# Graph message passing on one core: one gathered unit fewer in each round, two rounds more, and 5 of 21 key one-hots made by ScalarE

## The chip, the cores and the metric

The kernel runs on one core of a Trainium2 chip. The metric is the device time of one execution in microseconds (us); lower is better. The engines are named as the profile names them: PE is TensorE (PEld its weight loads), DVE is VectorE, ACT is ScalarE, POOL is GpSimd, SP is SyncE.

## The reference

```
x: [12500, 64]   src, dst: [400000], dst sorted ascending   edge_attr: [400000, 64]   edge_weight: [400000, 1]
h   = x @ node_w.T
rf  = edge_attr @ review_w.T
m   = (h[src] + rf) * edge_weight
agg = segment_sum(m, dst, 12500)
out = layernorm(x + agg)          # over the 64 features
```

Since both products are linear, the kernel first sums `weight * x[src]` and `weight * edge_attr` per destination node into `sums` (128 partitions: 64 features of x, 64 of edge_attr; one column per node), and multiplies by the two weight matrices once at the end.

## The kernel before

**Two ways to sum x[src].** Edges are sorted by destination. For the first 90 units of 2048 edges (`ROUNDS * GATHERED` = 18 x 5) the rows `x[src]` are gathered from memory by indirect DMA, 16 DMAs of 128 rows to a unit, issued by POOL (`gather_tiles`, L534). PE then sums the gathered rows and the unit's edge_attr rows with a weighted one-hot (`sum_g`), and DVE adds the result to `sums` (`add_g`). For the nodes of all later edges nothing of x is gathered. Those nodes are taken three at a time, as a *span*: one run of 128 edges per span. DVE makes two one-hots of the run (`make_hot`): `hot_key`, 128 edges x 294 keys (L854), where the key is `(src >> 7) * 3 + (dst - first node)`, and `hot_lo`, the low 7 bits of src times the weight, in two parts (L855). PE multiplies them (`count_window`, L1425) into a table of weights per source and node, ACT copies two spans' tables from PSUM to `counts` (`read_counts`, L1240), and PE multiplies `counts` with the resident table of x (`sum_x`, L1438). DVE adds that into `sums` (`add_x`, L772). The edge_attr rows of these later edges come by plain DMAs in 106 units, six to a round (`SUMMED`), summed by `sum_a`, `multiply_a`, `add_a`.

**Rounds and steps.** A round is 6 steps (`RG`), a step is a group of 21 spans (`GW`). 18 rounds of 126 spans cover the last 6804 nodes, and 8 spare spans (`SPILLS`) take runs longer than 128 edges. Rounds run in a hardware loop of two rounds to an iteration, and the last two rounds stand outside it. Step g of a round multiplies counts of group g while the spans of group g+1 are made and counted; in steps 0 to 4 it also has one gathered unit, in every step one edge_attr unit.

**The order on each engine is written out by hand**, in `step_of` of each engine:

- PE: spans 0 to 20 of the next group, with `sum_g` ahead of span 4, `multiply_g` ahead of 8, `sum_a` ahead of 12, `multiply_a` ahead of 16, and a fifth of `sum_x` ahead of each of 4, 8, 12, 16 and 20. The small transposes (`turn_g`, `turn_a`, `turn_cols`) stand ahead of 8 in steps 1, 2 and 4.
- DVE: six spans ahead of PE, since each one-hot has six buffers (`HOT_BUFS`) and waits `counted` for the span six before; the step's other work (`make_g_hot`, `make_a_hot`, `make_..._slot_hot`, `add_g`, `add_a`) lies between the spans, and `add_x` ends the step.
- ACT: the 11 copies of a step (`read_counts`), with `copy_g` after the second, `copy_a` after the sixth, and once a round `compare` (step 0, L1215), `read_g`, `read_a` and `read_cols`. PE may not start a pair of spans before the copy of the pair two before is done.
- POOL: for the round after, `gather_row`, `gather_unit` 0, `gather_runs`, `gather_unit` 1 to 4, all in one queue. `gather_row` (L552) fetches the 128 edges that hold the begin of each run; it follows `find_rows` on DVE (L793, step 0) and `find_runs` on DVE (L802, step 1, ahead of the loop's k = 22) waits for it. `gather_unit` 0 also waits for `take_src` on DVE (L706, step 1, k = 14), and each unit waits until PE has summed the unit that held its buffer in the round before.

## Time and profile before

| what | value |
|---|---|
| time, median of 3 runs | 2291.5 us (2286.46 to 2296.65) |
| the profiled execution: its time | 2279.48 us |
| the profiled execution: its span | 2277.7 us |
| mean granted TensorE clock | 0.915 of full |
| busy DVE | 1986.1 us, 87% |
| busy PE | 1891.5 us, 83% |
| busy POOL | 1674.5 us, 74% |
| busy ACT | 962.4 us, 42% |
| instructions | 93210 |

The span is the time from the first to the last instruction. A busy share counts only the time within instructions: POOL, in a row of indirect DMAs, is not busy in the pause between two of them, and matmuls overlap, so a busy PE is not one at its peak. "Issue" is time in which an engine waited for nothing that the profile shows. Rows of a timeline give start, duration, engine, line, instruction, and in brackets the idle time before and what ended it.

### The profile page before, as it was taken

What the parts mean: (1) busy time and instruction counts of PE and PEld (TensorE: products, weight loads), DVE (VectorE), ACT (ScalarE), POOL (GpSimd) and SP (SyncE); (2) the same over time, 40 slices, a digit from 0 to 9 for tenths busy, and PEclk for the clock granted to TensorE, in tenths of its full rate; (3) what the DMA queues carried; (4) which work ended last, traced back from release to release, by engine and by line L of the source; (5) the groups of instructions that cost most, each with busy time, mean ns of one, the idle gap of its engine ahead of it and who ended that gap; (6) DMA issues with size and microseconds to landing.
All of it is one profiled execution on the core that took longest, in us unless ns stands there. A gap on an engine that the chain in (4) does not pass through costs nothing.

```text
span 2277.7 us, 93210 instructions
## 1 busy us (share of the span) xinstructions
PE 1891.5 (83%) x35999; PEld 1641.8 (72%) x36000; DVE 1986.1 (87%) x6206; ACT 962.4 (42%) x1602; POOL 1674.5 (74%) x1539
## 2 busy tenths in 40 slices
PE   1659788979897989898998899789988998989974
PEld 1557677767776777777777778677777877877864
DVE  3969898989898989898998899889988998989974
ACT  0324344444344444444443445344434443444434
POOL 3777777777777777777777777777777777777700
PEclk8679998999898999999998999899988998989997
DMA  6224333433333333333333333333433333433302
GB/s 139 55 59 86 72 79 79 83 72 83 78 74 76 84 77 84 76 84 77 84 76 76 76 85 80 75 72 84 84 75 69 82 79 71 84 73 72 66 3 57
DMA packets 480104, 173.08 MB, mean 76 GB/s; under 512 B 443549, under 2 KB 455397, under 8 KB 479445
## 3 DMA queue, kind: packets, MB, share of 16 engines
q1 hardware_dynamic: 426791, 111.57, 22.8%
q0 software_dynamic: 49632, 51.95, 11.4%
q8 instruction: 314, 5.14, 1.0%
q10 hardware_dynamic: 3218, 3.20, 0.7%
q14 instruction: 149, 1.22, 0.2%
HBM read 163.39 MB, written 3.20 MB: 73 GB/s over the span
## 4 chain that ended last, share of the span: by engine, by line
POOL 67%; issue 20%; DVE 7%; PE 2%; DMA 1%; ACT 1%; DVEq 0%; POOLq 0%; ACTq 0%; SPq 0%
POOL rows L534 64%; DVE hot_lo L855 3%; DVE hot_key L854 2%; DMA counts<-dst 1%; POOL run_src L560 1%; POOL run_dst L560 1%; POOL run_w L560 1%; POOL dst_row L552 1%; PE x_ps L1438 1%; ACT x_tab L1308 1%; DMA dst_row<-dst,row_i 0%; PE count_ps L1425 0%; DVE packed L990 0%; PE count_ps L1451 0%; DVE x_tab L1010 0%
## 5 line engine op out<-in xcount | busy, mean ns | idle before, releaser
L534 POOL DMA_INDIRECT rows<-x,g_src_cols x1440 | 1584.3, 1100 | 443.6 <-issue 438.7
L1240 ACT ACTIVATE counts<-count_ps 128x588 f32<-128x588 f32 (+1 forms) x1192 | 851.9, 750 | 1138.3 <-PE count_ps L1425 1127.5
L1425 PE MATMUL count_ps<-hot_key,hot_lo 128*128 128x294 f32 x4552 | 897.9, 330 | 257.2 <-DVE hot_lo L855 213.0
L855 DVE SCALAR_TENSOR_TENSOR hot_lo<-count,cols 128x256 fp32r<-128x256 f16 x2276 | 1078.6, 474 | 0.0
L1425 PEld LDWEIGHTS count_ps<-hot_key,hot_lo 128*128 128x128 f32 x4552 | 673.6, 196 | 386.7 <-DVE hot_lo L855 247.5
L854 DVE TENSOR_SCALAR hot_key<-count,cols 128x294 fp32r<-128x294 f16 x2276 | 864.5, 380 | 47.8 <-PE count_ps L1425 27.7
L1438 PE MATMUL x_ps<-counts,x_tab 128*64 128x63 f32 x21364 | 800.2, 229 | 41.3 <-DVE sums L772 41.2
L1438 PEld LDWEIGHTS x_ps<-counts,x_tab 128*64 128x64 f32 x21364 | 725.6, 142 | 102.5 <-DVE sums L772 48.0
L1352 PE MATMUL unit_ps<-rows,g_hot 128*32 128x64 f32 x5760 | 120.8, 246 | 0.0
L1352 PEld LDWEIGHTS unit_ps<-rows,g_hot 128*32 128x32 f32 x5760 | 104.4, 127 | 18.2 <-issue 18.2
L802 DVE TENSOR_SCALAR off<-dst_row,b_all 126x128 f32<-126x128 int32 x18 | 5.2, 290 | 116.4 <-DMA dst_row<-dst,row_i 116.4
L662 POOL TENSOR_TENSOR x_tab<-x_tab,counts 128x512 f32<-128x512 f32 (+1 forms) x6 | 5.5, 937 | 91.7 <-DVE counts L1021 91.7
L1352 PE MATMUL unit_ps<-rows,a_hot 128*32 128x64 f32 x3392 | 69.3, 222 | 0.0
L1352 PEld LDWEIGHTS unit_ps<-rows,a_hot 128*32 128x32 f32 x3392 | 52.2, 109 | 17.7 <-issue 17.7
L772 DVE TENSOR_TENSOR sums<-sums,x_ps 64x63 f32 (+1 forms) x216 | 47.0, 218 | 13.2 <-PE x_ps L1438 6.3
L1223 ACT ACTIVATE g_slots<-unit_ps 128x128 f32<-128x128 f32 x90 | 25.0, 278 | 58.9 <-PE unit_ps L1352 58.9
L1389 PE MATMUL window_bank<-a_slot_hot,a_slots 128*64 128x128 f32 x212 | 45.8, 298 | 0.0
L744 DVE TENSOR_SCALAR a_slot_hot<-column,a_slot_dst 128x128 f32<-128x128 f32 x106 | 40.6, 383 | 3.3
L1381 PE MATMUL window_bank<-g_slot_hot,g_slots 128*128 128x128 f32 x180 | 36.3, 283 | 0.0
L552 POOL DMA_INDIRECT dst_row<-dst,row_i x18 | 18.3, 1017 | 24.3 <-DVE row_i L796 19.1
L1451 PE MATMUL count_ps<-w_t,sums 128*128 128x128 f32 x196 | 24.9, 296 | 12.8 <-DVEq L1187 12.8
L1451 PEld LDWEIGHTS count_ps<-w_t,sums 128*128 128x128 f32 x196 | 24.8, 212 | 12.9 <-DVEq L1187 12.9
(196 smaller groups left out, 728.3 us busy)
## 6 DMA issues: line engine op xcount, KB each, us to landing
rows<-edge_attr SPq DMA_DIRECT2D x196, 512.0 KB
rows<-x,g_src_cols POOLq DMA_INDIRECT x1440
out<-x_tab SPq DMA_DIRECT2D x12, 256.0 KB
counts<-dst SPq DMA_DIRECT2D x1, 848.0 KB
a_stage<-dst SPq DMA_DIRECT2D x17, 48.0 KB
a_stage_w<-edge_weight SPq DMA_DIRECT2D x17, 48.0 KB
g_stage<-src SPq DMA_DIRECT2D x18, 40.0 KB
g_stage<-dst SPq DMA_DIRECT2D x18, 40.0 KB
```

What stands on the lines that cost most here:

```text
L534: pool.indirect_dma_start(out=g_x[:, i, t, :], out_offset=None, in_=x, in_offset=bass.IndirectOffsetOnAxis(ap=g_src_cols[at.p][:, k:k + 1] ...
L552: pool.indirect_dma_start(out=dst_row[:, :], out_offset=None, in_=dst.rearrange("(a b) -> a b", b=P), in_offset=bass.IndirectOffsetOnAxis( ...
L560: pool.indirect_dma_start(out=tile, out_offset=None, in_=dram.rearrange("(a b) -> a b", b=1), in_offset=bass.IndirectOffsetOnAxis(ap=index ...
L772: made = dve.tensor_tensor(to, to, x_ps[half * F:(half + 1) * F, 0:NS], ALU.add)
L854: dve.tensor_scalar(hot_key[h][:, :], count16[:, :], cols_[:, KEY, j:j + 1], None, ALU.is_equal)
L855: dve.scalar_tensor_tensor(hot_lo[h][:, :, :], count16[:, 0:P].unsqueeze(1).to_broadcast([P, 2, P]), cols_[:, LO, j:j + 1], cols_[:, W_LOW ...
L1240: act.activation(to, count_ps[(g + e) % 2][:, 0:n, 0:KEYS].rearrange("p a (h d) -> p a h d", d=D), ACT.Copy).then_inc(counts_read, 1)
L1352: done = pe.matmul(to[j * PAD:(j + 1) * PAD, :], hot[:, at:at + PAD], tiles[:, q * QUADS + j, :], start=(q == 0), stop=(q == STACK - 1))
L1389: pe.matmul(a_window_ps, a_slots[:, :], a_slot_hot[:, :], start=True, stop=True).then_inc(a_multiplied, 1)
L1425: done = pe.matmul(count_ps[(g + e) % 2][:, k % 2, 0:KEYS], hot_lo[h][:, i, :], hot_key[h][:, :], start=(i == 0), stop=(i == 1))
L1438: done = pe.matmul(x_ps[half * F:(half + 1) * F, 0:n], x_tab[:, hi, :], counts[:, g % 2, hi, 0:n], start=(hi < 2), stop=(hi >= HI - 2))
L1451: last = pe.matmul(out_ps[n % 2][:, i, :], sums[:, (h0 + i) * P:(h0 + i + 1) * P], w_t[:, :], start=True, stop=True)
```

## The change

`ROUNDS` goes from 18 to 20 and `GATHERED` from 5 to 4. So 80 units of edges are gathered instead of 90, the edge_attr units that are not gathered go from 106 to 116 (two of them in the last round, where there were four), and 2528 spans are counted instead of 2276. In each step, five of the 21 spans (1, 5, 9, 13 and 17) get their `hot_key` from ACT: `far_key = |count - key|` in one activation (Abs, with the negated key as bias), then `hot_key = relu(1 - far_key)` in a second (Relu, with a column of ones as bias), which waits for the first. DVE leaves out L854 for these spans and still makes their `hot_lo`. `read_cols` writes the negated keys once a round, and PE waits for `act_key_ready` besides `hot_ready` ahead of these spans. ACT makes the key of span 2e+6 or 2e+7 behind the copy of pair e.

```diff
--- before.py
+++ after.py
@@ -34,11 +34,12 @@
 D = 3
 GW = 21
 RG = 6
-ROUNDS = 18
-GATHERED = 5
+ROUNDS = 20
+GATHERED = 4
 SUMMED = 6
 SPILLS = 8
 HOT_BUFS = 6
+ACT_KEYS = (1, 5, 9, 13, 17)
 ATTR_BUFS = 2
 NOWHERE = 1000.0
 
@@ -156,6 +157,8 @@
         KEY, LO, W_LOW, W_TOP = range(CELLS)
         packed = sb("packed", [P, CELLS, P])
         cols = [sb(f"cols{b}", [P, CELLS, RW]) for b in range(2)]
+        neg_key = [sb(f"neg_key{b}", [P, RW]) for b in range(2)]
+        far_key = sb("far_key", [P, KEYS], F16)
         hot_key = [sb(f"hot_key{b}", [P, KEYS], F32R) for b in range(HOT_BUFS)]
         hot_lo = [sb(f"hot_lo{b}", [P, 2, P], F32R) for b in range(HOT_BUFS)]
 
@@ -303,6 +306,8 @@
         added = sem("added")
 
         hot_ready = sem("hot_ready")
+        far_made = sem("far_made")
+        act_key_ready = sem("act_key_ready")
         counted = sem("counted")
         counts_read = sem("counts_read")
         x_summed = sem("x_summed")
@@ -851,7 +856,8 @@
                     dve.wait_ge(cols_ready, at.r + g // RG + 1)
                 if not isinstance(n, int) or n >= HOT_BUFS:
                     dve.wait_ge(counted, n - HOT_BUFS + 1)
-                dve.tensor_scalar(hot_key[h][:, :], count16[:, :], cols_[:, KEY, j:j + 1], None, ALU.is_equal)
+                if k not in ACT_KEYS:
+                    dve.tensor_scalar(hot_key[h][:, :], count16[:, :], cols_[:, KEY, j:j + 1], None, ALU.is_equal)
                 dve.scalar_tensor_tensor(
                     hot_lo[h][:, :, :], count16[:, 0:P].unsqueeze(1).to_broadcast([P, 2, P]), cols_[:, LO, j:j + 1],
                     cols_[:, W_LOW:W_TOP + 1, j].unsqueeze(2).to_broadcast([P, 2, P]), ALU.is_equal, ALU.mult
@@ -1205,8 +1211,41 @@
             def read_cols(q, p, n=RW):
 
                 act.wait_ge(turned, q + 1)
+                act.activation(neg_key[p][:, 0:n], turn_ps[:, KEY * n:(KEY + 1) * n], ACT.Copy, scale=-1.0)
                 act.activation(cols[p][:, :, 0:n], turn_ps[:, 0:CELLS * n].rearrange("p (q t) -> p q t", q=CELLS), ACT.Copy
                                ).then_inc(cols_ready, 1)
+
+            def keys_before(at, g, k):
+
+                return (at.r * RG + g) * len(ACT_KEYS) + sum(i < k for i in ACT_KEYS)
+
+            def make_key(at, g, k):
+
+
+                h, j = (g * GW + k) % HOT_BUFS, (g % RG) * GW + k
+                n, made = first(at, g) + k, keys_before(at, g, k)
+                neg = neg_key[at.p if g < RG else 1 - at.p]
+                if g % RG == 0 and k == ACT_KEYS[0]:
+                    act.wait_ge(cols_ready, at.r + g // RG + 1)
+                if not isinstance(n, int) or n >= HOT_BUFS:
+                    act.wait_ge(counted, n - HOT_BUFS + 1)
+                if not isinstance(made, int) or made >= 1:
+                    act.wait_ge(act_key_ready, made)
+                act.activation(far_key[:, :], count16[:, :], ACT.Abs, bias=neg[:, j:j + 1]).then_inc(far_made, 1)
+                act.wait_ge(far_made, made + 1)
+                act.activation(hot_key[h][:, :], far_key[:, :], ACT.Relu, bias=all_ones[:, 0:1], scale=-1.0
+                               ).then_inc(act_key_ready, 1)
+
+            def keys_after(at, g, e):
+
+
+                for ahead in (2 * e + HOT_BUFS, 2 * e + HOT_BUFS + 1):
+                    at_g, at_k = g + ahead // GW, ahead % GW
+                    over = isinstance(at.r, int) and at.r * RG + at_g > ROUNDS * RG
+                    if e == EVACS - 1 and ahead > 2 * e + HOT_BUFS:
+                        continue
+                    if at_k in ACT_KEYS and not over and at_k < windows_of(at, at_g):
+                        make_key(at, at_g, at_k)
 
             def compare(q):
 
@@ -1259,8 +1298,12 @@
             act.wait_ge(tables_ready, 1)
             with act.If(is_narrow(act) == 1):
                 read_cols(0, 0)
+                for w in ACT_KEYS:
+                    if w < HOT_BUFS:
+                        make_key(Round(0, 0), 0, w)
                 for e in range(EVACS):
                     read_counts(Round(0, 0), 0, e)
+                    keys_after(Round(0, 0), 0, e)
 
                 def step_of(at, g):
 
@@ -1270,6 +1313,12 @@
                     for e in range(EVACS):
                         if e < evacs:
                             read_counts(at, c, e)
+                            if not (last and c == RG):
+                                keys_after(at, c, e)
+                            else:
+                                for ahead in (2 * e + HOT_BUFS, 2 * e + HOT_BUFS + 1):
+                                    if ahead in ACT_KEYS and ahead < SPILLS:
+                                        make_key(at, c, ahead)
                         if e == 1 and g < GATHERED:
                             copy_g(at, g)
                         if e == 2 and g == 0 and not last:
@@ -1417,6 +1466,8 @@
                 n, h = first(at, g) + k, (g * GW + k) % HOT_BUFS
                 e = k // 2
                 pe.wait_ge(hot_ready, n + 1)
+                if k in ACT_KEYS:
+                    pe.wait_ge(act_key_ready, (at.r * RG + g) * len(ACT_KEYS) + ACT_KEYS.index(k) + 1)
                 if k % 2 == 0:
                     before = evacs_before(at, g) + e
                     if not isinstance(before, int) or before >= 2:
```

## Rows read from the trace of the kernel before

**Rows 1.** The page: busy time of each engine, and the chain by engine.

```profile
PE 1891.5 (83%) x35999; PEld 1641.8 (72%) x36000; DVE 1986.1 (87%) x6206; ACT 962.4 (42%) x1602; POOL 1674.5 (74%) x1539
...
POOL 67%; issue 20%; DVE 7%; PE 2%; DMA 1%; ACT 1%; DVEq 0%; POOLq 0%; ACTq 0%; SPq 0%
```

**Rows 2.** Waits, all engines: total us, times, longest.

```profile
POOL rows L534 <- issue: 438.7, 1439, 0.3
...
DVE off L802 <- DMA dst_row<-dst,row_i: 116.4, 18, 21.3
```

**Rows 3.** Groups by line: count, busy us, mean ns, idle before.

```profile
L534 POOL DMA_INDIRECT rows<-x,g_src_cols x1440 | 1584.3, 1100 | 443.6 <-issue 438.7 <-DVE g_src_cols L706 4.9
...
L855 DVE SCALAR_TENSOR_TENSOR hot_lo<-count,cols 128x256 fp32r<-128x256 f16 x2276 | 1078.6, 474 | 0.0
...
L1240 ACT ACTIVATE counts<-count_ps 128x588 f32<-128x588 f32 (+1 forms) x1192 | 851.9, 750 | 1138.3 <-PE count_ps L1425 1127.5
...
L854 DVE TENSOR_SCALAR hot_key<-count,cols 128x294 fp32r<-128x294 f16 x2276 | 864.5, 380 | 47.8 <-PE count_ps L1425 27.7 <-issue 18.7 <-ACT cols L1208 0.7
...
L1215 ACT ACTIVATE compared<-sample_tab,bias_all 126x1696 bf16<-126x1696 int16 x18 | 30.4, 1691 | 0.0
...
L1308 ACT ACTIVATE x_tab<-x_tab,counts 128x64 f32<-128x64 f32 x56 | 13.4, 333 | 0.0
...
L1195 ACT ACT_TABLE_LOAD x1 | 1.3, 1283 | 6.3 <-PE turn_ps L1322 6.3
```

**Rows 4.** VectorE timeline, markers of a round (start us, us, engine line).

```profile
45.97 0.29 DVE L802 TENSOR_SCALAR off<-dst_row,b_all 126x128 f32<-126x128 int32 x1 [5.97 <-DMA dst_row<-dst,row_i]
...
98.33 0.15 DVE L793 TENSOR_SCALAR less<-less 126x1 f32<-126x1 f32 x1 [1.13 <-ACT compared L1215]
...
145.76 0.29 DVE L802 TENSOR_SCALAR off<-dst_row,b_all 126x128 f32<-126x128 int32 x1 [21.27 <-DMA dst_row<-dst,row_i]
...
1994.25 0.14 DVE L793 TENSOR_SCALAR less<-less 126x1 f32<-126x1 f32 x1
...
2028.99 0.29 DVE L802 TENSOR_SCALAR off<-dst_row,b_all 126x128 f32<-126x128 int32 x1 [8.66 <-DMA dst_row<-dst,row_i]
```

**Rows 5.** VectorE timeline, the adds that end a step.

```profile
1045.45 0.21 DVE L772 TENSOR_TENSOR sums<-sums,x_ps 64x63 f32 x1
...
1069.34 0.47 DVE L772 TENSOR_TENSOR sums<-sums,x_ps 64x63 f32 x2
...
1108.36 0.21 DVE L772 TENSOR_TENSOR sums<-sums,x_ps 64x63 f32 x1
...
1125.80 0.21 DVE L772 TENSOR_TENSOR sums<-sums,x_ps 64x63 f32 x1
...
1145.39 0.21 DVE L772 TENSOR_TENSOR sums<-sums,x_ps 64x63 f32 x1
...
1161.58 0.47 DVE L772 TENSOR_TENSOR sums<-sums,x_ps 64x63 f32 x2
```

**Rows 6.** VectorE timeline, consecutive instructions.

```profile
1071.78 0.36 DVE L854 TENSOR_SCALAR hot_key<-count,cols 128x294 fp32r<-128x294 f16 x1
1072.07 0.47 DVE L855 SCALAR_TENSOR_TENSOR hot_lo<-count,cols 128x256 fp32r<-128x256 f16 x1
1072.46 0.26 DVE L715 TENSOR_TENSOR g_hot<-column,g_cols 128x112 f32<-128x112 f32 x1
```

**Rows 7.** Windows, one step: length, then busy of PE, PEld, DVE, ACT, POOL.

```profile
874.25:891.71 17.46, 16.37 (x352) 14.08 (x343) 17.23 (x53) 8.23 (x14) 13.50 (x14) 1.00 0.43 89
```

**Rows 8.** TensorE timeline, start of a step.

```profile
873.36 1.11 PE L1352 MATMUL unit_ps<-rows,g_hot 128*32 128x64 f32 x64
874.78 1.38 PE L1438 MATMUL x_ps<-counts,x_tab 128*64 128x63 f32 x38 [0.30 <-DVE sums L772]
876.08 1.35 PE L1425 MATMUL count_ps<-hot_key,hot_lo 128*128 128x294 f32 x8
877.27 0.39 PE L1381 MATMUL window_bank<-g_slot_hot,g_slots 128*128 128x128 f32 x2
```

## The prediction

> **What bounds the kernel now.** I read the page first. VectorE (DVE) has the highest busy share, 87%, TensorE (PE) has 83%, GpSimd (POOL) 74% [rows 1]. But the chain that ended last runs through POOL for 67% of the span and through "issue" for another 20% [rows 1]. The list of waits explains the second part: POOL's gathers were preceded 1439 times by some 0.3 us of issue, 438.7 us in all [rows 2]. Busy and idle of L534 together are 1584.3 + 443.6 = 2027.9 us over 1440 gathers, 1.408 us each [rows 3]. So POOL has no free time, although its busy share says a quarter. A round of POOL is 80 gathers and 4 small ones, which I price alike: 84 x 1.408 = 118.3 us. The markers of a round on DVE give the same: from the first L793 of the loop to the last there are 16 rounds in 1994.25 - 98.33 = 1895.9 us, 118.5 us each [rows 4].
>
> Who pays is seen in DVE's wait at L802 for the row gather, which stands behind all gathers of the round before in POOL's queue: 116.4 us in 18 waits [rows 2]. Of these 5.97 us lie before and 8.66 us behind the 16 rounds, so 101.8 us lie within them [rows 4]. Without these waits the round would have been (1895.9 - 101.8) / 16 = 112.1 us. This is the pace of DVE with PE close behind it, and POOL hides it. So the kernel has two bounds, 118.3 us (POOL) and 112.1 us (DVE), and both must fall for the time to fall per round. The change adds two rounds: it has to win more than a tenth of each round to win at all.
>
> In the 112.1 us there is one more thing. The step at the seam of the hardware loop, from 1045.45 to 1069.34, takes 23.9 us [rows 5], against some 17.5 us for its kind; a plain step with a gathered unit takes 17.44 us (1108.36 to 1125.80) and the last step of a round, which has no gathered unit, 16.19 us (1145.39 to 1161.58) [rows 5]. So a seam costs 6.4 us in every second round, or 3.2 us a round. I leave it as it is: nothing in the change touches it, and the number of seams rises with the rounds.
>
> **The change part by part.**
>
> *Gathers.* A round has 64 instead of 80: (64 + 4) x 1.408 = 95.7 us on POOL. The first gathered unit of the next round also waits for the source columns (L706, step 1, k = 14); from there POOL needs 95.7 us up to and with the next row gather, and L802 of the next round stands 8 spans behind that round's L706. So POOL stalls nobody so long as a round is longer than about 96 us. It will then wait for DVE, not DVE for it. The wait of 5 to 6 us a round at L802 goes away; what is late next is DVE's own sequence. The start fits too: the first big wait, 21.27 us at 145.76 [rows 4], was for 80 gathers behind each other; 16 fewer end 22.5 us earlier.
>
> *Keys on DVE.* In a row of spans, L855 starts 0.29 us after L854, and the next instruction 0.39 us after L855 [rows 6]; the means of 380 and 474 ns [rows 3] hold overlap at their ends. A removed key is worth the spacing, 0.29 us. 30 keys a round: 8.7 us. Bounds: 0.38 us, its whole duration, if nothing overlapped (11.4 us a round), and 0.21 us, if two L855 in a row can't overlap (0.29 less 0.474 - 0.39), 6.3 us.
>
> *One gathered unit less on DVE.* The steps with and without it differ by 17.44 - 16.19 = 1.25 us [rows 5].
>
> So DVE's pace is 112.1 - 8.7 - 1.25 = 102.2 us a round.
>
> *PE.* Its work in a span, a portion of `sum_x` and so on is unchanged in a round, and it loses the sums of one gathered unit. In the step from 874.25 to 891.71 it is busy for 16.37 of 17.46 us at a granted clock of 1.00 [rows 7], but that contains stretches in which it waited for DVE within a group. From the starts: a portion of `sum_x` takes 1.30 us (874.78 to 876.08), four spans 1.2 us (876.08 to 877.27), a gathered unit 1.1 us (873.36, then 0.30 us idle before 874.78) [rows 8]. Five portions, 21 spans at 0.30 to 0.32 us, 1.1, and about 1.1 us of smaller products and switches give 15.1 to 15.5 us, an estimate of the floor of a step; 16.37 is the ceiling. DVE's plain step becomes 17.44 - 5 x 0.29 = 16.0 us. So the two engines, a tenth apart before, are nearly level afterwards, and each will sometimes wait for the other across the six buffers.
>
> *Keys on ACT.* The trace has no Abs or Relu. Its two rows with a per-partition operand are 64 columns in 333 ns and 1696 columns in 1691 ns [rows 3]; between them 0.832 ns a column, so 294 columns take 524 ns. The second activation waits for the first, so a key takes 1.05 us; the bounds are 0.9 us, if the activations overlap at their ends by 0.08 us as DVE's instructions do [rows 6], and 1.3 us, if each hand-over costs another 0.1 us. A step has 5 keys, 5.3 us. ACT was busy for 8.23 us in a step [rows 7], so 13.5 us of 16.0 us, and 15.4 us in step 0 with `compare` (1.69 us and its read-out). It holds, but it is no longer free at once when PE has counted a pair. The place that I expect to matter: the key behind the copy of pair 8 puts 1.05 us between the copies of pairs 8 and 9, and PE needs the copy of pair 9 for the first pair of the next step, after one portion of `sum_x` and one span (1.6 us). ACT needs 0.2 + 0.7 + 1.05 + 0.7 us from the count of pair 8, PE arrives 0.65 + 1.6 us after it: 0.4 us short. In DVE's pace this lies in time that PE has left (16.0 less 15.5 us). The negated keys, one activation of some 0.3 us a round, are on no path.
>
> The rule of the Trainium skill, "ScalarE: Activation LUTs", section "Rules for kernel authors", speaks against such a move: relu and the like belong on VectorE, not on ScalarE. The rows bear out its premise, 0.29 us on DVE against about 1.05 us on ACT for a key; by it alone the change would cost 0.76 us for each of 600 keys, 456 us of engine time, but on an engine with more than half of its time free [rows 1]. The sum goes by which engine sets the step.
>
> *Coupling.* For DVE and PE being level, for ACT's copies coming later, for `compare` coming later to L793 (DVE waited 1.13 us there already [rows 4]) I put 1.5 us a round on top. Bounds: 0, as everything now goes by DVE, and 6 us, 1 us a step, if PE stands at its ceiling of 16.37 us and ACT's 0.4 to 0.6 us come on top. I take the low part, since a step of PE at its ceiling contains waits that go with DVE's pace. The round is then 103.7 us.
>
> **The sum.** Before: 98.3 us to the first L793, 16 x 118.5 = 1895.9, and 283.5 us from the last L793 to the end (2277.7 - 1994.25); together 2277.7. After: the start falls by 1.3 us (five keys of the first group go to ACT), 97.0. Then 18 rounds of 103.7 us, 1866.6. The last part loses the wait of 8.66 us at 2028.99 [rows 4], some 60 keys (17.4 us) and two edge_attr units of the last round (4 x 0.6 us and their tail, 2 us net), and gains the coupling of nearly two rounds: 283.5 - 8.7 - 17.4 - 2.0 - 2.5 for the two gathered units + 2.5 = 255.4 us. Span: 2219 us. About 2 us lie around the span (2279.48 against 2277.7), and the median of the runs is 13.8 us above the span before; at the same ratio, 1.0061, the median after is 2232 us. In short form the span is 145 + 20 x round, and it equals that of before at a round of 106.6 us.
>
> **The rivals.**
>
> *TensorE becomes the bound.* Against it: DVE's list of waits holds little for PE in plain steps, and its step of 17.44 us is far above PE's floor. For it: 16.37 us busy at full clock [rows 7] is above the new 16.0 us. Six steps at 16.4 to 16.5 us, with DVE's long steps (1 and 4) unchanged, add about 2 us: a round of 105.5 us, 2269 us. If it is a little more, 106.6 us, nothing is gained.
>
> *ScalarE's keys hold up TensorE's copies: slower.* One mechanism: PE must wait for the copy of pair 9 (and in step 0 for that of pair 3 behind `compare`), falls behind DVE, and DVE waits for `counted`. The price is what exceeds PE's reserve. From 0.8 us a step on (106.6 less 102.2 over six steps, rounded up) the change is lost; at 1.15 us a step the round is 109 us and the time 2339 us. For it: ACT's share in step 0 is 15.4 of 16 us. Against: ACT falls behind by 0.4 to 0.6 us in my sum, once a step, and catches up.
>
> *Table loads.* If Abs or Relu were not in the loaded set, two loads of 1.283 us [rows 3] would come with every key: 77 us a round, ACT would then set a round of some 160 us, and the time would be over 3300 us. The trace shows one load for Identity, Copy and Sign together, at L1195, and says nothing of the other two. The Trainium skill, "ScalarE: Activation LUTs", section "Table sets: the hidden batching unit", says that relu and abs are in every set; by that this rival is out.
>
> *The relief is larger.* The removed key is worth 0.38 us, or DVE never waits for PE, because with the row waits gone PE keeps the granted clock of 1.00 that it has in the plain step [rows 7], where its mean is 0.915. The round is 100 to 101 us and the time 2160 to 2180 us.
>
> *No relief.* POOL stays the bound: only if a gather became slower than 1.408 us by a tenth or more, which nothing here suggests, since it waits for neither DVE nor data.
>
> **How the numbers follow.** DVE sets the pace with some coupling (2202 to 2268 us, round 102.2 to 105.5): 0.60, likeliest 2232. TensorE sets it, still faster (about 2269): 0.14. Between (round 106.0 to 107.2): 0.05. ScalarE holds up TensorE (about 2339): 0.09. Larger relief (about 2180): 0.10. Table loads or POOL: 0.02. A difference of under 0.5%, 11 us, is about what a measurement of this kernel can't tell from no change; that is 2280 to 2303 us. Faster: 0.60 + 0.14 + 0.10 = 0.84; same 0.05; slower 0.11. The range is 2185 to 2295 us: it leaves out the larger half of the larger relief and the slower cases, less than 0.2 together.
>
> **What the profile would show.** Right: DVE's wait at L802 near zero; POOL idle some 5 us or more in each round, waiting for L706; L854 1926 times, L855 2528 times, 0.39 us apart where they follow each other; a round of 102 to 105 us from L793 to L793; the activations at 0.52 us each; no further table load; ACT busy near 75%; a plain step near 16 us; PE's granted clock above 0.915, as the long waits are gone. Wrong: a plain step above 17 us with DVE waiting for `count_ps` in every step, and PE waiting for ACT's `counts` or keys: then the coupling was the term that failed. If L855 behind L855 takes 0.47 us, it was the key's price. If the seam's cost grows, because ACT now restarts late as well, it was the term that I left unchanged.

## The result, and the profile after

The changed kernel takes 2263.84 us (median of 4 runs, 2262.61 to 2268.77), the kernel before 2289.68 us (median of 4). The ratio on record is 0.9895, 95% interval 0.9865 to 0.9925; the two medians alone give 0.9887. It is faster, and the time lies in the range, but the gain is 1.05% where 2.6% was forecast. The profiled execution has a span of 2266.8 us; the sum had said 2219.

The page after, busy shares and the chain by engine, against [rows 1]:

```profile
PE 1983.5 (88%) x38569; PEld 1752.4 (77%) x38570; DVE 1987.5 (88%) x6186; ACT 1578.5 (70%) x2973; POOL 1703.4 (75%) x1387
...
DVE 39%; PE 29%; issue 16%; POOL 5%; DVEq 4%; ACT 4%; DMA 2%; ACTq 0%; SPq 0%; POOLq 0%
```

The chain moved from POOL (67%) to DVE and PE (39% and 29%). From this alone one would say that POOL is out of it. The groups by line say otherwise, against [rows 3]:

```profile
L539 POOL DMA_INDIRECT rows<-x,g_src_cols x1280 | 1605.7, 1254 | 406.5 <-issue 383.1 <-DVE g_src_cols L711 22.2 <-DVE row_i L801 1.2
...
L861 DVE SCALAR_TENSOR_TENSOR hot_lo<-count,cols 128x256 fp32r<-128x256 f16 x2528 | 1165.8, 476 | 0.1
...
L860 DVE TENSOR_SCALAR hot_key<-count,cols 128x294 fp32r<-128x294 f16 x1926 | 722.6, 375 | 73.5 <-PE count_ps L1476 72.1 <-ACT cols L1215 0.9
...
L1236 ACT ACTIVATE hot_key<-far_key,all_ones 128x294 fp32r<-128x294 f16 x602 | 326.1, 542 | 19.6
...
L1234 ACT ACTIVATE far_key<-count,neg_key 128x294 f16<-128x294 f16 x602 | 316.2, 525 | 0.1
```

Each gather of x rows became longer: 1254 ns in the mean instead of 1100. Busy and idle are now 1605.7 + 406.5 us; without the 23.4 us in which POOL waited for L711 and L801 that is 1.55 us a gather instead of 1.41, 10% more. 64 gathers and 4 small ones are then 105.6 us, where 95.7 us was forecast. The waits, against [rows 2]:

```profile
DVE hot_key L860 <- PE count_ps L1476: 72.1, 40, 6.3
...
DVE off L807 <- DMA dst_row<-dst,row_i: 67.5, 12, 15.0
...
DVE less L798 <- ACT compared L1254: 30.5, 20, 6.1
...
POOL rows L539 <- DVE g_src_cols L711: 22.2, 19, 5.2
```

The wait for the row gather, now L807, is 67.5 us instead of 116.4; it was to vanish. POOL itself waited only 22.2 us in all for DVE (L711), about 1 us a round: it has almost no slack. The markers of a round (L798, L793 before), against [rows 4]:

```profile
92.42 0.15 DVE L798 TENSOR_SCALAR less<-less 126x1 f32<-126x1 f32 x1 [0.95 <-ACT compared L1254]
...
960.48 0.15 DVE L798 TENSOR_SCALAR less<-less 126x1 f32<-126x1 f32 x1 [1.42 <-ACT compared L1254]
...
1171.83 0.15 DVE L798 TENSOR_SCALAR less<-less 126x1 f32<-126x1 f32 x1 [1.42 <-ACT compared L1254]
...
2009.77 0.15 DVE L798 TENSOR_SCALAR less<-less 126x1 f32<-126x1 f32 x1 [1.21 <-ACT compared L1254]
```

From the first to the last there are 18 rounds in 1917.35 us, 106.5 us each; the forecast was 103.7. The two rounds in the middle, 960.48 to 1171.83, take 105.7 us each; over most of the kernel the rounds take 98.4 and some 113.4 us in turn, and the mean also holds two early ones of 115.2 and 117.3 us. Within the 18 rounds DVE waits 55.3 us for the row gather (67.48 less the first wait of 5.94 and the last of 6.20), 3.1 us a round. The adds that end a step, against [rows 5]:

```profile
946.26 0.47 DVE L777 TENSOR_TENSOR sums<-sums,x_ps 64x63 f32 x2
...
971.74 0.47 DVE L777 TENSOR_TENSOR sums<-sums,x_ps 64x63 f32 x2
...
1005.42 0.47 DVE L777 TENSOR_TENSOR sums<-sums,x_ps 64x63 f32 x2
...
1021.17 0.47 DVE L777 TENSOR_TENSOR sums<-sums,x_ps 64x63 f32 x2
...
1052.60 0.21 DVE L777 TENSOR_TENSOR sums<-sums,x_ps 64x63 f32 x1
...
1070.08 0.21 DVE L777 TENSOR_TENSOR sums<-sums,x_ps 64x63 f32 x1
```

A plain step takes 15.75 us (1005.42 to 1021.17), even less than the 16.0 us of the forecast. The step at the seam of the loop takes 25.48 us (946.26 to 971.74), against 17.48 us for the same step without a seam (1052.60 to 1070.08). This seam is the shortest of the eight within the loop; their mean is 26.0 us.

### The profile page after: what moved, and what is told of

Its sections match the earlier page's. It is cut to its first block, busy times and chain, and to the rows that moved or that the text cites. A ratio compares the mean times of both kernels' runs of the same rounds, so it can differ in the third digit from the quotient of the medians.

```text
span 2266.8 us, 102339 instructions
## 1 busy us (share of the span) xinstructions
PE 1983.5 (88%) x38569; PEld 1752.4 (77%) x38570; DVE 1987.5 (88%) x6186; ACT 1578.5 (70%) x2973; POOL 1703.4 (75%) x1387
## 4 chain that ended last, share of the span: by engine, by line
DVE 39%; PE 29%; issue 16%; POOL 5%; DVEq 4%; ACT 4%; DMA 2%; ACTq 0%; SPq 0%; POOLq 0%
DVE hot_lo L861 19%; PE count_ps L1476 12%; PE x_ps L1489 12%; DVE hot_key L860 11%; POOL rows L539 5%; PE unit_ps L1401 4%; DMA dst_row<-dst,row_i 2%; ACT compared L1254 1%; DVEq L764 1%; DVE sums L777 1%; ACT counts L1279 1%; DMA counts<-dst 1%; DVEq L858 1%; DVE sums L767 1%; DVEq L755 1%
## 5 line engine op out<-in xcount | busy, mean ns | idle before, releaser
L539 POOL DMA_INDIRECT rows<-x,g_src_cols x1280 | 1605.7, 1254 | 406.5 <-issue 383.1
L1279 ACT ACTIVATE counts<-count_ps 128x588 f32<-128x588 f32 (+1 forms) x1324 | 922.4, 744 | 550.6 <-PE count_ps L1476 547.0
L861 DVE SCALAR_TENSOR_TENSOR hot_lo<-count,cols 128x256 fp32r<-128x256 f16 x2528 | 1165.8, 476 | 0.1
L1476 PEld LDWEIGHTS count_ps<-hot_key,hot_lo 128*128 128x128 f32 x5056 | 727.5, 193 | 280.9 <-issue 110.1
L1489 PE MATMUL x_ps<-counts,x_tab 128*64 128x63 f32 x23716 | 871.2, 226 | 20.1 <-DVE sums L777 20.0
L1489 PEld LDWEIGHTS x_ps<-counts,x_tab 128*64 128x64 f32 x23716 | 788.8, 139 | 87.4 <-issue 33.0
L860 DVE TENSOR_SCALAR hot_key<-count,cols 128x294 fp32r<-128x294 f16 x1926 | 722.6, 375 | 73.5 <-PE count_ps L1476 72.1
L1236 ACT ACTIVATE hot_key<-far_key,all_ones 128x294 fp32r<-128x294 f16 x602 | 326.1, 542 | 19.6
L1234 ACT ACTIVATE far_key<-count,neg_key 128x294 f16<-128x294 f16 x602 | 316.2, 525 | 0.1
L1401 PE MATMUL unit_ps<-rows,g_hot 128*32 128x64 f32 x5120 | 105.6, 243 | 0.0
L807 DVE TENSOR_SCALAR off<-dst_row,b_all 126x128 f32<-126x128 int32 x20 | 5.6, 281 | 67.5 <-DMA dst_row<-dst,row_i 67.5
L767 DVE TENSOR_TENSOR sums<-sums,window_bank 64x128 f32 x116 | 33.9, 293 | 4.1
L1438 PEld LDWEIGHTS window_bank<-a_slot_hot,a_slots 128*64 128x64 f32 x232 | 22.2, 134 | 19.7 <-issue 19.7
L1254 ACT ACTIVATE compared<-sample_tab,bias_all 126x1856 bf16<-126x1856 int16 x20 | 36.5, 1825 | 0.0
```

The lines of the kernel that those rows point to most:

```text
L539: pool.indirect_dma_start(out=g_x[:, i, t, :], out_offset=None, in_=x, in_offset=bass.IndirectOffsetOnAxis(ap=g_src_cols[at.p][:, k:k + 1] ...
L860: dve.tensor_scalar(hot_key[h][:, :], count16[:, :], cols_[:, KEY, j:j + 1], None, ALU.is_equal)
L861: dve.scalar_tensor_tensor(hot_lo[h][:, :, :], count16[:, 0:P].unsqueeze(1).to_broadcast([P, 2, P]), cols_[:, LO, j:j + 1], cols_[:, W_LOW ...
L1234: act.activation(far_key[:, :], count16[:, :], ACT.Abs, bias=neg[:, j:j + 1]).then_inc(far_made, 1)
L1236: act.activation(hot_key[h][:, :], far_key[:, :], ACT.Relu, bias=all_ones[:, 0:1], scale=-1.0).then_inc(act_key_ready, 1)
L1254: act.activation(compared[:, :], sample_tab[0:RW, :], ACT.Sign, bias=bias_all[:, bass.ds(q, 1)], accum_out=less[:, 0:1]).then_inc(compared ...
```

## Where the gathers lose their time

The lengths of single gathers in the trace after fall into groups: most of 0.94 to 1.1 us, then 78 between 1.7 and 2.9 us, and 39 of more than 5 us, 19 of them in step 4, 19 in step 5 (one each in 19 of the 20 rounds) and one near the start. One of them, from step 5, on POOL, and the two instructions on DVE near its end (start us, us, engine, line):

```profile
933.97 6.22 POOL L539 DMA_INDIRECT rows<-x,g_src_cols  x1 [0.30 <-issue]
...
939.11 0.27 DVE L720 TENSOR_TENSOR a_hot<-column,a_cols 128x112 f32<-128x112 f32 x1
...
939.41 0.28 DVE L722 TENSOR_TENSOR a_hot<-a_hot,a_cols 128x112 f32<-128x112 f32 x1
```

L722 waits for L720, so DVE is idle for 0.03 us ahead of it (instructions that follow each other without a wait overlap by some 0.1 us instead). The gather ends at 940.19 us, 0.78 us after L722 starts. The same is found in the kernel before:

```profile
1180.18 3.11 POOL L534 DMA_INDIRECT rows<-x,g_src_cols  x1 [0.30 <-issue]
...
1182.21 0.26 DVE L715 TENSOR_TENSOR g_hot<-column,g_cols 128x112 f32<-128x112 f32 x1
...
1182.50 0.28 DVE L717 TENSOR_TENSOR g_hot<-g_hot,g_cols 128x112 f32<-128x112 f32 x1
```

It ends at 1183.29 us, 0.79 us after the start of L717. Of the 117 long gathers after and the 78 before (over 1.7 us), 116 and 77 end 0.7 to 0.8 us after the start of an instruction of DVE that follows an idle gap (L717, L706, L753 and L762 before; the last three read PSUM). For gathers below 1.3 us such an instruction lies 0.45 to 0.95 us ahead of the end in only 260 of 1358 cases before and 273 of 1120 after. So a long gather seemed to be waiting for DVE to pause. Step 4 has no gathered unit any more, so no `make_g_hot` and no `add_g` between its spans: from k = 6 to k = 18 twelve spans follow each other without a pause, where there were two pauses before. Step 5 never had a gathered unit, and its stream was as unbroken in the kernel before; what changed there is that keys left it.

## The experiments

Theory A: the gather is held up by DVE until DVE pauses. Theory B: the lengths come from POOL's own queue or place in the round. Theory C: the seams are on the path. Rival D to C: POOL takes it back. The ratios are those on record, to the kernel before as it ran beside each (medians of 2285.4 to 2289.7 us), with 95% intervals.

| run | what | time us | ratio | mean gather ns |
|---|---|---|---|---|
| change | | 2263.84 | 0.9895 (0.9865 to 0.9925) | 1254 |
| e1_rounds_only | rounds part alone | 2339.73 | 1.0230 (1.0196 to 1.0263) | 1148 |
| e2_keys_only | keys part alone | 2374.86 | 1.0389 (1.0345 to 1.0433) | 1173 |
| e3_pauses | change, 5 pauses in steps 4, 5 | 2226.42 | 0.9736 (0.9708 to 0.9764) | 1105 |
| e8_one_pause | change, 1 pause in steps 4, 5 | 2216.02 | 0.9697 (0.9666 to 0.9728) | 1168 |
| e10_no_pause | change, 5 waits without pause | 2264.49 | 0.9898 (0.9879 to 0.9917) | 1257 |
| e6_before_pauses | before, 4 pauses a step | 2235.95 | 0.9789 (0.9756 to 0.9822) | 1037 |
| e4_long_loop | change, 6 rounds an iteration | 2262.89 | 0.9906 (0.9873 to 0.9939) | 1264 |
| e5_both | e3 and e4 together | 2177.01 | 0.9523 (0.9495 to 0.9550) | 1104 |
| e7_compare_early | e5, compare moved ahead | 2172.86 | 0.9505 (0.9473 to 0.9536) | 1125 |
| e9_before_both | before, e6 and 4 rounds an iteration | 2214.11 | 0.9675 (0.9656 to 0.9695) | 1042 |
| e11_one_pause_all | e7 with 1 pause | 2165.45 | 0.9464 (0.9446 to 0.9482) | 1171 |

### Pauses in the streams of steps 4 and 5

```diff
+PAUSES = (8, 10, 12, 14, 16)
 # VectorE, step_of
                     for k in range(HOT_BUFS, GW + HOT_BUFS):
+                        if g >= GATHERED and k in PAUSES and not last:
+                            dve.wait_ge(hot_ready, first(at, c) + k)
```

> The changed kernel, but VectorE waits for its own previous hot_lo ahead of five of the spans (k = 8, 10, 12, 14, 16) in steps 4 and 5, which makes a pause of about 0.1 us each. Theory A: a gather gets in at any pause, so the gathers of 5.5 and 6.2 us shrink to under 3 us, the mean falls from 1.25 to about 1.12 us, the waits for the row gather (67.5 us) fall to some 25 us, those of the first rounds, and the time to about 2235 us, 0.976 of before. Theory B: gathers and time as in the changed kernel (0.9895), plus 1 us a round for the pauses.

Measured: 2226.42 us. The group of POOL's gathers, and two of the waits:

```profile
L540 POOL DMA_INDIRECT rows<-x,g_src_cols x1280 | 1414.5, 1105 | 544.2 <-issue 384.3 <-DVE g_src_cols L712 159.9
```

```profile
POOL rows L540 <- DVE g_src_cols L712: 159.9, 19, 15.3
...
DVE off L808 <- DMA dst_row<-dst,row_i: 20.9, 2, 15.0
```

Ten waits more a round on DVE made the kernel 37 us faster. All but one of the gathers above 5 us are gone (one of 12 us at the start is left), POOL has 159.9 us to wait for DVE, and the row gather is waited for in two early rounds only. Without the time in which POOL waited for DVE a gather now costs (1414.5 + 544.2 - 159.9) / 1280 = 1.405 us, the 1.408 us of the prediction. The round is 104.1 us (99.6 and 108.6, from L799 to L799), next to the forecast 103.7. The pauses have their price on DVE: each is an idle gap of 0.13 us, and steps 4 and 5 take 18.0 and 15.75 us instead of 16.8 and 14.65 to 14.85 us, some 2.2 us a round and not the 1 us that was expected.

### The same waits without a pause

```diff
-                            dve.wait_ge(hot_ready, first(at, c) + k)
+                            dve.wait_ge(hot_ready, first(at, c) + k - 2)
```

> The same five waits in steps 4 and 5 as in the first test with pauses, but each for the hot_lo two spans earlier, which is long done: the instructions and their number are the same, VectorE does not pause. Theory A (the pause lets the gather in): gathers of 5.5 and 6.2 us as in the changed kernel, time 0.99. Rival (the wait instructions themselves, or the shift in code, helped): 0.974.

```profile
L540 POOL DMA_INDIRECT rows<-x,g_src_cols x1280 | 1609.4, 1257 | 404.6 <-issue 383.4 <-DVE g_src_cols L712 20.0 <-DVE row_i L802 0.9
```

```profile
DVE off L808 <- DMA dst_row<-dst,row_i: 67.3, 12, 16.2
```

Measured: 2264.49 us, 39 gathers above 5 us, the wait for the row gather as in the changed kernel. With the same instructions and no pause nothing is gained. It is the pause that ends a gather's wait.

### One pause instead of five

`PAUSES = (12,)`.

> The changed kernel with a single pause, at k = 12 of steps 4 and 5. Theory A: any pause that comes in the stream ends a gather's wait, so the longest waits are halved, below 3.5 us, and the time is near that with five pauses (0.974), at most 0.98. If what matters is the whole of the pauses, and not one in the middle, 0.985 or more.

```profile
L540 POOL DMA_INDIRECT rows<-x,g_src_cols x1280 | 1494.9, 1168 | 454.1 <-issue 382.8 <-DVE g_src_cols L712 69.7 <-DVE run_i L814 0.6
```

Measured: 2216.02 us, 10 us better than with five. The gathers of 5.5 and 6.2 us are cut to 1.8 and 2.5 us; the mean is longer than with five pauses, but DVE loses less in the two steps (17.0 and 14.8 or 15.2 us instead of 18.0 and 15.7), and POOL is still just fast enough: the row gather is waited for about 1 us in every second round. The two runs were made on different chips, and the intervals of their ratios overlap, so that one pause is better than five is likely and not shown.

### Pauses in the kernel before

The same two lines in the kernel before, in all six steps, with `PAUSES = (7, 12, 17, 21)`.

> The kernel before, with nothing of the change, but VectorE waits for its own previous hot_lo ahead of the spans at k = 7, 12, 17 and 21 of each step. Theory A (a gather gets in only at a pause of VectorE) says that waits on VectorE make this kernel faster: the gathers of 2.1 to 3.1 us shrink, the mean falls from 1.10 to about 1.05 us, a round from 117.1 to about 114 us, where VectorE's own 112.1 us and 2.4 us of pauses set it; ratio about 0.98. Rival (the gathers' length has nothing to do with VectorE, the pauses in the other test worked by moving something else): no change, or slower by what the pauses cost, 1.00 to 1.02.

```profile
L535 POOL DMA_INDIRECT rows<-x,g_src_cols x1440 | 1493.6, 1037 | 472.5 <-issue 434.9 <-DVE g_src_cols L707 36.4 <-DVE row_i L797 0.9
```

Measured: 2235.95 us, ratio 0.9789. Against [rows 3] the mean fell from 1100 to 1037 ns, and 3 gathers instead of 78 are above 1.7 us. The round is 116.0 us instead of 118.5 (about 114 was expected), and DVE waits for the row gather in two early rounds only. A gather now costs (1493.6 + 472.5 - 36.4 - 0.9) / 1440 = 1.339 us: of the 1.408 us that the prediction took for POOL's own price, a part was already time held up by DVE. In a kernel that POOL bounds, waits on an engine that is 87% busy are worth 2.1%, twice what the whole change is. Theory A stands for the kernel before as well.

### The rounds part alone

`ACT_KEYS = ()`: 20 rounds of 4 gathered units, all keys on DVE.

> 20 rounds with 4 gathered units, all keys on VectorE (the rounds part of the change alone). Theory of the sum: VectorE's work is about 106.5 us a round (107.8 before less 1.25), with seams and compare about 111 us, POOL free; time about 2385 us, 1.04 of before. Theory A (a gather is held up by VectorE's streams with lone L861 behind each other): no gather above 3.6 us here, mean back at 1.10 us. Theory B (the long gathers come from POOL's own queue with 64 gathers a round, or from steps 4 and 5 having no gathered unit): two gathers of 5 to 6 us a round here too, mean 1.25 us. The seam: if the keys on ScalarE made it dearer, TensorE's issue pause at it is back at some 4.6 us; if not, 6.8 us.

```profile
L539 POOL DMA_INDIRECT rows<-x,g_src_cols x1280 | 1470.1, 1148 | 613.0 <-issue 382.5 <-DVE g_src_cols L711 229.0 <-DVE row_i L801 0.9
```

Measured: 2339.73 us, ratio 1.023. POOL waits 229.0 us for L711: here DVE sets the pace, 110.5 us a round (106.7 and 114.2 in turn). The round is as expected, the time 45 us below the 2385 us that were made of it. Neither theory was right about the gathers. Theory A expected none above 3.6 us: there are 18 above 5 us (16 of them 6.4 us) with all keys on DVE. Theory B expected two in each round and a mean of 1.25 us: there is one, and the mean is 1148 ns. 16 of the 18 lie in step 4, the step that lost its pauses. Step 5, whose stream is without a pause for its first 8.4 us here and in the kernel before, has one above 5 us in 20 rounds here and none there. So a stream without a pause is not enough by itself. As to the seam: TensorE's pauses at it (`count_ps`, issue) come to 5.1 us in the mean, against 6.5 us in the changed kernel, and the step at it takes 7.1 us more than without a seam, against 8.6 us. The keys on ACT made the seam dearer.

### The keys part alone

18 rounds of 5 gathered units, keys of five spans on ACT; `compared` and `far_key` share memory, for space, with two more waits on ACT.

```diff
-ROUNDS = 20
-GATHERED = 4
+ROUNDS = 18
+GATHERED = 5
-        compared = sb("compared", [RW, SAMPLES], BF16)
+        scratch = sb("scratch", [P, SAMPLES + KEYS % 2], BF16)
+        compared = scratch[0:RW, 0:SAMPLES]
-        far_key = sb("far_key", [P, KEYS], F16)
+        far_key = scratch[:, 0:KEYS].bitcast(F16)
```

> 18 rounds with 5 gathered units, keys of 5 spans on ScalarE (the keys part alone; the scratch of compare and far_key share memory, for space, which adds a short wait on ScalarE). The kernel stays bound by POOL, so VectorE's 8.7 us a round give nothing: 1.00. By theory A the lone L861 make the streams harder to get into, the gathers longer and the kernel slower: mean above 1.15 us, 84 gathers a round, 4 us or more a round, 1.02 to 1.04.

```profile
L540 POOL DMA_INDIRECT rows<-x,g_src_cols x1440 | 1689.4, 1173 | 443.3 <-issue 438.6 <-DVE g_src_cols L712 4.7
```

```profile
DVE off L808 <- DMA dst_row<-dst,row_i: 343.4, 18, 33.7
```

Measured: 2374.86 us, ratio 1.0389, and the wait for the row gather is 343.4 us against 116.4 [rows 2]. DVE's work fell and the kernel became 3.9% slower: 80 gathers x 0.073 us are 5.8 us a round, times 18 some 105 us; the span grew by 96 us. The forecast of theory A, 1.02 to 1.04, held. Neither part is a gain by itself. Together they are, since the one takes gathers off POOL and the other work off DVE.

The two halves also tell where each long gather comes from. Mean gather in ns, and in brackets how many are above 5 us, sorted by the step in which the gather starts (from the timelines of POOL and DVE):

| run | step 4 | step 5 |
|---|---|---|
| before | 1118 (0) | 1042 (0) |
| rounds part alone | 1736 (16) | 1109 (1) |
| keys part alone | 1151 (0) | 1832 (17) |
| change | 1764 (19) | 1807 (19) |

The gather in step 5 of the keys part alone is that of the changed kernel, and it ends behind the same instruction of DVE (L723 here, L722 there):

```profile
1200.05 6.21 POOL L540 DMA_INDIRECT rows<-x,g_src_cols  x1 [0.30 <-issue]
...
1205.48 0.28 DVE L723 TENSOR_TENSOR a_hot<-a_hot,a_cols 128x112 f32<-128x112 f32 x1
```

In step 5 of the kernel before, beside an equally unbroken stream, the gathers pass:

```profile
1263.81 1.03 POOL L534 DMA_INDIRECT rows<-x,g_src_cols  x1 [0.30 <-issue]
1265.15 1.05 POOL L534 DMA_INDIRECT rows<-x,g_src_cols  x1 [0.30 <-issue]
1266.51 1.06 POOL L534 DMA_INDIRECT rows<-x,g_src_cols  x1 [0.30 <-issue]
```

So each half of the change brings a long gather of its own: the missing unit the one in step 4, the moved keys the one in step 5. Together they hold POOL up for 9.7 us (5.5 and 6.2 us instead of some 1 us each), about the 9.9 us by which its round is over the forecast. Which property of the thinned stream does it, the runs do not separate: with three keys fewer among its twelve spans (k = 9, 13 and 17) a larger share of it is `hot_lo`, which has two inputs in SBUF, and its rhythm is another. In the kernel before the gathers in step 5 start 1.35 us apart, the length of two spans on DVE (0.28 and 0.40 us each), which would fit the rhythm; no run varied it.

### Six rounds to an iteration of the loop

```diff
-            with eng.Fori(0, ROUNDS // 2 - 1) as rr:
-                for p in range(2):
-                    do(Round(rr * 2 + p, p))
+            with eng.Fori(0, (ROUNDS - 2) // PER_LOOP) as rr:
+                for p in range(PER_LOOP):
+                    do(Round(rr * PER_LOOP + p, p % 2))
```

with `PER_LOOP = 6`.

> The changed kernel with six rounds to an iteration of the hardware loop instead of two: 2 seams inside the loop instead of 8. Theory C (a seam costs about 9.5 us, all of it on the path): 6 x 9.5 = 57 us less, 2207 us, 0.964. Rival D (with its long gathers POOL needs about 105 us a round, and takes back what the seams give): the waits for the row gather grow from 67 to over 110 us and the time stays at 2245 us or above, 0.98.

```profile
DVE off L808 <- DMA dst_row<-dst,row_i: 104.4, 18, 15.0
...
DVE hot_key L861 <- PE count_ps L1477: 33.9, 34, 5.4
```

Measured: 2262.89 us, 0.9906, no difference from the change. DVE waits less for PE (33.9 us, 72.1 before this edit), and the row gather's wait grows from 67.5 to 104.4 us. What six seams gave, POOL took. Rival D held: the time is the one that it forecast, the row gather's wait stayed a little under its 110 us.

> Pauses and the long loop together. If C and A both hold, neither POOL nor the seams are left: a round of about 98.5 us, 0.945 of before (2165 us). If only one holds, about what that one gives alone.

```profile
POOL rows L541 <- DVE g_src_cols L713: 105.6, 19, 13.4
...
DVE off L809 <- DMA dst_row<-dst,row_i: 18.4, 2, 12.5
```

Measured: 2177.01 us, 0.9523. With the pauses in, the long loop is worth 2226.42 - 2177.01 = 49.4 us, 8.2 us for each of the six seams. Theory C held too, once POOL was out of the way (9.5 us a seam and a round of 98.5 us were expected, the round is 99.5). What happens at a seam shows on TensorE in the changed kernel: a matmul of `count_ps` after 4.01 us of issue, and the next after 2.19 us:

```profile
948.98 0.57 PE L1476 MATMUL count_ps<-hot_key,hot_lo 128*128 128x294 f32 x1 [4.01 <-issue]
...
951.74 2.08 PE L1476 MATMUL count_ps<-hot_key,hot_lo 128*128 128x294 f32 x7 [2.19 <-issue]
```

No engine is waited for there. The pause is not all of the price: TensorE's granted clock, full in the window 944.0:948.9, is 0.50 of full (1.2 of 2.4 GHz) in 949.0:955.8, after the 4 us in which it did nothing, and seven of its matmuls take 2.08 us there where eight took 1.36 us before. The Trainium skill, "Runtime: NRT & Kernel Launch", section "Instruction fetch mechanics", says that a taken branch outside the fetched window forces a fetch before execution goes on; the rows agree in that the pause is "issue" and comes once a loop iteration, but no run here looked at the fetch itself.

### compare ahead of the keys

On ACT, `compare` after the copy of pair 1, ahead of the key of span 9 and of `copy_g`, instead of after the copy of pair 2.

> Five pauses, six rounds to an iteration, and compare ahead of the key of span 9 and of copy_g on ScalarE instead of behind them. VectorE's wait for compare, 1.3 us a round in the changed kernel, goes; 20 to 25 us less than without it if it is on the path: 0.942. If the later copies cost TensorE as much, 0.952 as without.

```profile
DVE less L800 <- ACT compared L1258: 6.2, 1, 6.2
```

Measured: 2172.86 us (2167.08 to 2175.43), 0.9505. DVE's wait for it is down to one of 6.2 us (17.6 us in 13 waits without the edit), but the time is only 4 us less, with intervals that overlap. 20 to 25 us were expected. Inconclusive: most of that wait was not on the path, or came back as a later copy.

### The kernel before with both remedies, and the best version

> The kernel before (18 rounds, 5 gathered, no keys on ScalarE) with both remedies: a pause at k = 7, 12, 17 and 21 of each step and four rounds to an iteration of the loop (3 seams within it instead of 7). It tells what the change itself is worth once both side effects are gone. Pauses alone gave 0.979, with POOL and VectorE about level there (114 us): fewer seams help VectorE alone, so 0.970 to 0.979. The changed kernel with both was at 0.952, so the change would be worth about 2.5 %.

Measured: 2214.11 us, 0.9675 (0.9656 to 0.9695), a little below the lower end of what was expected.

> The changed kernel, six rounds to an iteration, compare early, and a single pause at k = 12 of steps 4 and 5 instead of five. One pause was 10 us better than five with the short loop: 0.946.

Measured: 2165.45 us, 0.9464 (0.9446 to 0.9482), the fastest of all. In the same comparison the kernel before with both remedies had 2214.11 us, a ratio of 0.978. That is not all the change's: the one has one pause in two of its steps, six rounds to an iteration and compare moved, the other four pauses in each step, never tried with fewer, and four rounds to an iteration. With five pauses, six rounds and compare in its old place the changed kernel had 2177.01 us, 1.7% less than 2214.11. With pauses alone in both it is 2216.02 against 2235.95 us, 0.9%.

## Why the prediction was wrong

**What bounds the kernel: right.** POOL at 118.3 us a round hid DVE's 112.1 us. The keys alone, which shorten DVE, gave nothing but a loss, and the rounds alone shifted the bound to DVE. But the 118.3 us were not POOL's own: with pauses in DVE's stream the same gathers cost 1.339 us each.

**DVE's work: right.** 16.0 us were forecast for the plain step, 15.75 us measured. L861 behind L861 follows at 0.40 us, so that sign of an error in the key's price did not show. Five keys removed took 1.69 us from the step (17.44 to 15.75), 0.34 us each instead of 0.29, within the bounds of 0.21 to 0.38; for 30 keys that is 1.5 us a round more relief than forecast.

**ScalarE's keys: right in price.** 525 and 542 ns against 524; the loop holds no table load, ACT is busy for 70% where 75% was said. TensorE does wait more for ACT's copies (45.8 us in 146 waits, against 14.7 us in 27 before), but the slower rival is not what took the gain: with POOL freed, these waits were still 46.1 us and the round 104.1 us.

**The failed step: the gathers' price.** The prediction took 1.408 us a gather over to the changed kernel, 95.7 us a round, and concluded "POOL stalls nobody". Measured were 1.55 us and 105.6 us, and DVE still waits 3.1 us a round for the row gather. The rival "No relief" named the very threshold, a tenth, and was set aside because "nothing here suggests" it, "since it waits for neither DVE nor data". That sentence was wrong: a gather does wait for DVE, until DVE pauses. The trace before held the sign: 78 of 1440 gathers of 2.1 us and more, ending 0.8 us behind DVE's pauses, and a mean of 1100 ns where the usual gather took some 1040. Both parts of the change took something from the stream that had let gathers in, the pauses of step 4 and keys of step 5, and each brought a long gather in nearly every round. The first wait for the row gather, which was to vanish as well, was still 15.0 us. In the profiled execution the row wait is 3.7 us or more in every second round, and behind it TensorE's clock falls: it is 1.00 of full in the window 1083.0:1089.0, in which TensorE is busy for 2.90 of 6.00 us, and 0.50 in 1089.0:1095.8, and in the 5 us behind that DVE waits another 1.7 us for PE.

The pauses test this step by itself. Five in each of two steps brought the gather back to the assumed price, 1.405 against 1.408 us, and with it the wait for the row gather to two early rounds; the time was 2226.42 us, and with one pause 2216.02, beside the predicted 2232. That these are so close is partly luck, since the ten pauses cost DVE 2.2 us a round, which no term of the sum holds: without them the round would be 101.9 us, below the forecast. So the other terms together were too dear by nearly 2 us a round, and hid half of what the gathers cost.

The Trainium skill, "GPSIMD Engine Reference", section "Key points", says that GpSimd shares its SBUF interfaces with VectorE, with contention for instructions in a 2-port mode or with two SBUF inputs; "DMA: Bandwidth & Descriptors", section "SWDGE vs HWDGE vs iDMA", adds that GpSimd writes the descriptors for its own DMAs into SBUF, and that VectorE locks it out of there during a 2-port mode. The runs agree with the direction (1254 ns a gather without pauses, 1105 with them); in which mode VectorE's instructions ran, no run shows. It should have been weighed in the prediction, as a rule that spoke against keeping the gathers' price. What the runs show beyond it is that the hold-up can span many instructions of VectorE (6.22 us, where one takes 0.4 to 0.5) and ends at a pause.

**The seam: mis-sized, and touched by the change.** "I leave it as it is: nothing in the change touches it". The 6.4 us came from the shortest of the seven seams within the loop; their mean is 7.3 us (24.8 less 17.5). After, the mean over eight is 8.6 us (26.0 less 17.4), with the rounds part alone 7.1, and the long loop gives 8.2 us. So the keys on ACT make a seam some 1.3 to 1.5 us dearer, as the last sign of being wrong had it, and since the 112.1 us of the sum hold the old seams as they were, the sum is short by some 0.7 us a round.

**Coupling: too large.** 1.5 us a round was put on 102.2. With the pauses in, the round was 104.1, and 101.9 without their 2.2 us. Against 102.2 less the 1.5 us by which the keys gave more, 1.2 us are left for coupling and the dearer seam together, so some 0.5 us for coupling.

**TensorE's clock: right.** It was 0.949 of full in the mean against 0.915, with the waits for the row gather down from 116.4 to 67.5 us; 0.957 with the five pauses, 0.968 with the long loop as well. What the clock alone is worth, no run separates.

**What stays open.** Why most gathers pass at once and some, at steady places in the round, wait for a pause, and why the stream of step 5 holds one up once some of its keys are gone. The order in which DVE's instructions come, or their phase to POOL's, would have to be varied on its own.

## What to carry to other kernels

An engine's free time is not read from its busy share, and the price of its instruction is not a constant: look at the spread (mean against usual), and at what stands at the end of the long ones, before carrying it to a kernel in which another engine's stream changes. Where VectorE runs back to back for many instructions beside a GpSimd queue of gathers, one short wait in the middle can be worth more than the work that it delays. When a bound is lifted by one edit, measure the halves: here each half alone was a loss of 2 to 4%, the sum a gain of 1%, and the places of the long gathers tell which half brings which. And give the remedy to the kernel before as well: the changed kernel with one pause is 3% faster than the kernel before, but only 0.9% faster than the kernel before with pauses of its own.

## What the runs showed of the hardware that was not expected

A gather on GpSimd, normally 0.94 to 1.1 us, took up to 6.2 us in a round's steady state beside an unbroken stream of VectorE instructions, and ended 0.8 us after the start of the instruction behind VectorE's next idle gap, which can be as short as 0.03 us. An unbroken stream does not always do it: one of 8.4 us in the kernel before let every gather pass, and held one up for 6.2 us once three of its keys were made elsewhere. Ten gaps of 0.13 us a round brought the mean from 1254 to 1105 ns, the same waits without a pause left it at 1257. One pass over the seam of a hardware loop cost 8.2 us in a kernel with four busy engines; some 6 us of it are pauses of TensorE that no engine ends, and behind them its granted clock was 0.50 for 6.8 us.
